# Cross-attention stack on one core: a new table of offsets for the hand-written order of all engines

## The reference, cut to what matters

```python
def _mha(x, kv, Wq, Wk, Wv, mask, causal):          # layer 0
    ...
    energy = jnp.einsum('bhsk,bhtk->bhst', Q, K)
    lengths = jnp.sum(energy[:, :, 0, :] != 0, axis=-1)
    energy = jnp.where(cols[None, None, None, :] >= lengths[:, :, None, None], -jnp.inf, energy)
    ...
    score = jax.nn.softmax(energy / jnp.sqrt(dk), axis=-1)
    out = jnp.einsum('bhst,bhtk->bhsk', score, V) * m
x = _L0_xattn_ref(x, ctx_1024, ...)   # attention 0, 1, feed-forward 256
x = _L1_xattn_ref(x, ctx_1024, ...)   # attention 2, 3, feed-forward 1024
x = _L2_xattn_ref(x, ctx_1024, ...)   # attention 4, heads of 64
x = _L3_xattn_ref(x, ctx_1024, ...)   # attention 5
```

## Time and profile before

| | us |
|---|---|
| median of 3 runs (2370.58 to 2371.80) | 2371.69 |
| the profiled execution | 2374.75 |
| its span, first to last instruction | 2373.0 |
| TensorE busy in it | 2331.2 |
| VectorE busy | 1498.0 |
| ScalarE busy | 1375.0 |
| GpSimd busy | 946.8 |

### The profile page before, as it was taken

The page is one execution under the profiler, slowest core; times in us unless marked ns, Lnnn a source line. Parts: engine busy times, 40 slices in busy tenths (PEclk is TensorE's granted clock), DMA queues, the critical chain, the costliest instruction groups (busy, mean ns, idle before and its releaser), DMA issues.

```text
span 2373.0 us, 74113 instructions
## 1 busy us (share of the span) xinstructions
PE 2331.2 (98%) x30353; PEld 1973.8 (83%) x30353; DVE 1498.0 (63%) x3091; ACT 1375.0 (58%) x3238; POOL 946.8 (40%) x1764
## 2 busy tenths in 40 slices
PE   8999999999999999999999999999999999999998
PEld 7788888888778888888877888888887788888887
DVE  6886654446888664444688766444478877544456
ACT  5566655545557665554655766554465675655545
POOL 3465422223457532223345743222334574322233
PEclk9999999999999999999999999999999999999999
DMA  5300000000100000000010000000001000000000
GB/s 184 111 2 3 2 2 1 1 1 16 40 5 2 3 2 2 1 1 1 18 40 3 2 3 3 1 1 1 1 24 34 2 2 3 2 1 2 1 1 20
DMA packets 23793, 32.51 MB, mean 14 GB/s; under 512 B 2304, under 2 KB 22176, under 8 KB 23328
## 3 DMA queue, kind: packets, MB, share of 16 engines
q1 hardware_dynamic: 23456, 27.78, 3.6%
HBM read 23.57 MB, written 4.19 MB: 12 GB/s over the span
## 4 chain that ended last, share of the span: by engine, by line
PE 90%; issue 4%; POOL 3%; DVE 2%; ACT 1%; DMA 0%; POOLq 0%; SPq 0%; DVEq 0%; ACTq 0%
PE M L582 52%; PE SC L778 14%; PE M L588 10%; PE M L812 6%; PE SC L794 3%; PE M L829 3%; PE SC L626 2%; POOL Kx L1339 1%; POOL Y L1375 1%; DVE nmax L1218 0%; ACT Pr L975 0%; POOL rstd L1390 0%; POOL q L1326 0%; POOL seen_diag L1366 0%; DVE Kx L1197 0%
## 5 line engine op out<-in xcount | busy, mean ns | idle before, releaser
L582 PE MATMUL M<-XT,W 128*128 128x128 f32 x4096 | 522.6, 277 | 1.0 <-DMA W<-w_k 0.9
L582 PEld LDWEIGHTS M<-XT,W 128*128 128x128 f32 x4096 | 491.5, 192 | 13.2 <-issue 2.0
L1218 DVE TENSOR_REDUCE nmax<-SC 128x8 f32<-128x1024 f32 x320 | 389.9, 1218 | 129.6 <-PE SC L778 129.3
L1339 POOL TENSOR_SCALAR Kx<-K,own,k_ones 128x128 f32<-128x128 f32 x640 | 294.4, 473 | 289.7 <-PE SC L778 214.0
L984 ACT ACTIVATE Pr<-SC 128x1024 f32<-128x1024 f32 x256 | 262.5, 1025 | 202.2 <-PE SC L778 201.3
L778 PE MATMUL SC<-Kx,Qx 32*128 32x128 f32 x5120 | 365.4, 280 | 13.7 <-issue 9.7
L778 PEld LDWEIGHTS SC<-Kx,Qx 32*128 32x128 f32 x5120 | 316.6, 186 | 68.1 <-issue 50.5
L778 PE MATMUL SC<-Qx,Kx 32*128 32x128 f32 x5120 | 372.2, 283 | 0.0
L954 ACT ACTIVATE Qx<-M,q_bias,q_scale 128x128 f32<-128x128 f32 x640 | 240.3, 457 | 148.1 <-PE M L582 148.1
L778 PEld LDWEIGHTS SC<-Qx,Kx 32*128 32x128 f32 x5120 | 310.9, 186 | 2.2 <-issue 0.7
L1414 POOL TENSOR_TENSOR Pr<-Pr,wrec 128x1024 f32<-128x1024 f32 x64 | 124.2, 1940 | 431.7 <-DVE wrec L1233 431.7
(11 more groups left out here) (145 smaller groups left out, 4074.2 us busy)
## 6 DMA issues: line engine op xcount, KB each, us to landing
X<-x SPq DMA_DIRECT2D x32, 128.0 KB, 2.1
c_in<-ctx_in SPq DMA_DIRECT2D x32, 128.0 KB, 2.3
out<-X SPq DMA_DIRECT2D x32, 128.0 KB, 1.7
RV<-row_vec SPq DMA_DIRECT2D x1, 2304.0 KB, 9.2
W<-w_k SPq DMA_DIRECT2D x5, 256.0 KB, 3.9
W<-w_q SPq DMA_DIRECT2D x5, 256.0 KB, 4.2
W<-w_v SPq DMA_DIRECT2D x5, 256.0 KB, 4.2
W<-w_f SPq DMA_DIRECT2D x1, 1024.0 KB, 6.2
```

The source lines that it names most:

```text
L582: last = pe.matmul(dst, a, b, start=(k == 0), stop=(k == len(lhsTs) - 1))
L1218: dve.tensor_reduce(nm, SC[h][:, :].rearrange("p (g c t) -> p g c t", c=KC, t=P), AX_X, ALU.max, negate=True).then_inc(maxima, 1)
L1339: last = pool.tensor_scalar(kx[:, half_of, c * P:(c + 1) * P], k[:, c * P:(c + 1) * P], own[:, half_of:half_of + 1], k_ones[:, half_of, c: ...
```

## The change

Only the numbers in `NARROW`, `OWN` and `BROAD` are new; the same instructions run, with the same waits, in other orders on TensorE, VectorE, ScalarE and GpSimd. On SyncE only the order in which DMAs stand can depend on slot times, and no offset of SyncE is changed. The diff, cut to two of the five narrow attentions:

```diff
-OWN = {0: dict(max=0.11, rXT=0.08, V=0.46, q0=-0.77, residual=2.68, exp=0.13, rE1=0.13, keys=-1.48, rPV=-0.16, K=-1.05,
-               rV=-0.08, MT=1.36, rK=0.06, rMT=-0.14, rQ=-0.03, XT=-1.497, L=-0.4, PV=2.951, seen0=-1.1, Q=-0.77,
-               CT=0.887, LN=3.34, LNe=0.34, rL=0.01, seen1=4, E1=3.08, rCT=0.02),
+OWN = {0: dict(XT=-1.456, rXT=-0.187, seen0=-1.418, CT=2.116, rCT=0.016, K=-1.012, rK=-0.393, keys=-0.654, Q=-0.714,
+               rQ=-0.106, V=-0.33, rV=0.231, q0=-0.946, L=-0.448, rL=0.15, max=0.108, exp=0.005, MT=1.188, rMT=-0.048,
+               PV=2.498, rPV=-0.2, E1=2.71, rE1=0.054, residual=2.874, LN=3.452, LNe=0.548, seen1=4.56),
...
-       2: dict(Q=-0.58, PV=2.56, rPV=0.34, rK=0.03, rV=0.14, V=0.163, keys=-0.92, rQ=0.05, LNe=0.38, max=0.08, K=-0.84,
-               rXT=0.03, MT=0.897, E3=3.68, E1=3.02, XT=-1.383, exp=0.06, rE2=0.07, E2=3.371, rMT=-0.07, LN3=0.14,
-               rCT=0.13),
+       2: dict(XT=-2.306, rXT=0.12, K=-1.158, rK=0.088, keys=-0.592, Q=-0.682, rQ=0.01, V=-0.288, rV=-0.152, max=-0.02,
+               exp=0.084, MT=1.006, rMT=0.026, PV=2.482, rPV=-0.032, E1=2.784, rE1=-0.04, E2=3.368, rE2=0.036, E3=4.26,
+               rE3=0.034, LN3=0.054, LNe=0.11),
...
```

More of the change, by code:

```diff
@@ L112, in wide @@
     return att(n) == WIDE
[L115 to L119, removed]
@@ L120 @@
-OWN = {0: dict(max=0.11, rXT=0.08, V=0.46, q0=-0.77, residual=2.68, exp=0.13, rE1=0.13, keys=-1.48, rPV=-0.16, K=-1.05,
-               rV=-0.08, MT=1.36, rK=0.06, rMT=-0.14, rQ=-0.03, XT=-1.497, L=-0.4, PV=2.951, seen0=-1.1, Q=-0.77,
-               CT=0.887, LN=3.34, LNe=0.34, rL=0.01, seen1=4, E1=3.08, rCT=0.02),
[L123 to L126, removed]
-       2: dict(Q=-0.58, PV=2.56, rPV=0.34, rK=0.03, rV=0.14, V=0.163, keys=-0.92, rQ=0.05, LNe=0.38, max=0.08, K=-0.84,
-               rXT=0.03, MT=0.897, E3=3.68, E1=3.02, XT=-1.383, exp=0.06, rE2=0.07, E2=3.371, rMT=-0.07, LN3=0.14,
-               rCT=0.13),
[L130 to L140, removed]
+NARROW = dict(XT=-1.2, TM=-1.5, SM=-1.25, K=-0.92, Q=-0.86, L=-0.42, V=0.3, CT=0.4, MT=0.86, PV=2.66, E1=3.2,
+              E2=3.54, E3=3.74, XF=4.4, F1=4.62, F2=4.9, seen0=-1.15, seen1=3.66, keys=-0.88, q0=-0.78,
+              mask_row=-0.3, residual=3.3, LN=3.4, T=1.5, H=0.5, rXT=0.03, rCT=0.03, rK=0.03, rQ=0.03, rL=0.03,
+              rV=0.03, rMT=0.03, rPV=0.03, rE1=0.03, rE2=0.03, rE3=0.03, rF1=0.03, rF2=0.03, max=0.12, exp=0.12,
+              LNe=0.25, LN3=0.06, LNf=0.05, rXF=0.03)
@@ new lines @@
+OWN = {0: dict(XT=-1.456, rXT=-0.187, seen0=-1.418, CT=2.116, rCT=0.016, K=-1.012, rK=-0.393, keys=-0.654, Q=-0.714,
+               rQ=-0.106, V=-0.33, rV=0.231, q0=-0.946, L=-0.448, rL=0.15, max=0.108, exp=0.005, MT=1.188, rMT=-0.048,
+               PV=2.498, rPV=-0.2, E1=2.71, rE1=0.054, residual=2.874, LN=3.452, LNe=0.548, seen1=4.56),
+       1: dict(XT=-1.496, rXT=0.293, TM=-2.964, SM=-2.156, K=-1.388, rK=0.258, keys=-1.056, Q=-0.622, rQ=-0.086,
+               V=-0.098, rV=0.06, q0=-0.946, L=-0.404, rL=0.064, max=0.068, exp=0.226, MT=1.15, rMT=0.134, PV=2.428,
+               rPV=-0.036, E1=2.926, rE1=-0.03, residual=2.9, LN=3.476, LNe=0.448, XF=3.948, rXF=0.12, F1=4.42,
+               rF1=-0.006, F2=4.798, rF2=-0.042, LNf=0.08),
+       2: dict(XT=-2.306, rXT=0.12, K=-1.158, rK=0.088, keys=-0.592, Q=-0.682, rQ=0.01, V=-0.288, rV=-0.152, max=-0.02,
+               exp=0.084, MT=1.006, rMT=0.026, PV=2.482, rPV=-0.032, E1=2.784, rE1=-0.04, E2=3.368, rE2=0.036, E3=4.26,
+               rE3=0.034, LN3=0.054, LNe=0.11),
+       3: dict(F2=5.282, XT=-2.294, rXT=0.009, mask_row=-1.232, K=-1.694, rK=0.074, keys=-0.238, Q=-0.936, rQ=0.046,
+               V=-0.098, rV=-0.33, max=-0.03, exp=0.086, MT=1.064, rMT=-0.186, PV=2.418, rPV=-0.036, E1=2.676, rE1=0.01,
+               E2=3.248, rE2=-0.02, E3=4.086, rE3=0.063, LN3=0.1, LNe=0.096, XF=4.61, rXF=-0.124, F1=4.958, rF1=0.003,
+               rF2=0.119, LNf=0.746),
+       5: dict(XT=-2.382, rXT=-0.084, K=-1.208, rK=0.156, keys=-0.784, Q=-0.834, rQ=-0.028, V=1.292, rV=0.06, max=0.144,
+               exp=-0.035, MT=1.076, rMT=0.01, PV=2.316, rPV=-0.134, E1=2.89, rE1=-0.006, E2=3.074, rE2=-0.022, E3=3.694,
+               rE3=0.021, LN3=0.242, LNe=0.528)}
@@ L143 @@
+BROAD = dict(XT=-1.398, Q=-0.354, Q1=0.142, K=-0.678, K1=0.284, S=0.028, S1=0.458, V=1.158, V1=0.912, TP=1.068,
+             TP1=1.23, PV=1.352, PV1=1.512, E3=2.14, sums=0.676, sums1=1.146, scale=0.57, scale1=1.186,
+             rXT=-0.138, rK=0.122, rQ=0.206, rV=0.074, rTP=-0.046, rPV=-0.025, max=0.12, exp=0.267, rE3=0.052,
+             LNe=0.618, LN3=0.122, rK1=0.136, rQ1=-0.034, rV1=0.108, rTP1=-0.008, rPV1=0.274, max1=0.24,
+             exp1=0.422)
 SETUP = {"ln1b": ("BT", "ln1b"), "f0": ("BC", "f0"), "lnfb": ("BT", "lnfb"), "q2": ("BC", "q2"), "k2": ("BC", "k2"),
```

## The result

| | before | after |
|---|---|---|
| median of 4 runs, us | 2371.23 | 2317.86 |
| lowest and highest | 2370.58, 2371.80 | 2317.53, 2318.61 |
| the profiled execution | 2374.75 | 2318.61 |
| its span | 2373.0 | 2316.8 |
| TensorE idle in the span | 41.8 | 18.2 |

The ratio is 0.9775, with a 95% interval of 0.9759 to 0.9792: 53.4 us faster by the medians, 56.1 by the two profiled executions. The prediction was 2329, with a range of 2307 to 2358.

What follows compares the result with a forecast made beforehand. The prediction took TensorE as the bound, VectorE next. From the profiled execution's 2374.75 it took 17.5 for fewer shape changes, 13.3 for L and 12 for other pauses, giving 2332.0; less 3.06, 2329 us, range 2307 to 2358.

Steps and rivals of the forecast that it cites:

- Part one: TensorE's queue: fewer returns from narrow pieces to whole-array work, 478 before and 389 after, saving 17.5 us.
- pieces next to pieces cost nothing: TensorE's queue: two kinds of narrow work in a row add no cost, read from PV taking 1.01 either way.
- Part two: L on TensorE waits for `q` from GpSimd, 15.3 us in all; about 2 stay, so 13.3 us go.
- Part three: TensorE's other pauses, 35.7 us, limited by VectorE: a third goes, -12 us, with bounds 0 and -35.7.
- the 92%: Attentions 0 and 1: TensorE assumed to wait once VectorE passes 92% busy, so 3.7 of 90 us can go.
- Moves with one answer: Side effects on PV, score steps, K copies, XT and SyncE loads, each checked against its cover and taken at zero.
- the 28 places with a cover of .07: Attention 0: 28 PVs stand 1.37 behind the step and need 1.3 for the exponentials; loss taken at zero.
- SyncE's late x loads: Attention 0: 12 x loads queue late behind CT, cover .7; taken at zero, 16 us at most.
- A: Rival: TensorE's pauses nearly all go, only 4 at the start and the tail's 2.8 stay; 2307 us, chance .15.
- B: Rival: pauses only change place, and the mode changes alone are left as gain; 2354 us, chance .15.
- C: Rival: slower than before, since PV waits for late exponentials on ScalarE, .53 at 58 PVs; 2385 us, chance .10.
- D: Rival: VectorE becomes slower with GpSimd working beside L1197, the length chain's end, costing 10 us; 2339 us, chance .10.

Runs made afterwards that it cites:

- x_l1: The new kernel with L of attention 1 alone moved up (offset -.56 for -.404): 2369.12 us, ratio 0.9988 to the kernel before.
- x_dve1: The new kernel with layer norm statistics done once more on VectorE in the 96 layer norms of attentions 0 and 1: 2321.60 us, ratio 0.9789.
- x_pvback: The new kernel with PV put back right behind the step at n + 2.5 in all narrow attentions: 2390.64 us, ratio 1.0079 to the kernel before.
- x_m5: The kernel before with the new offsets of attention 5 alone: 2421.09 us, ratio 1.0204.
- x_m0125: The kernel before with the new offsets of attentions 0, 1, 2 and 5, the old ones in attention 3 and the wide one: 2395.28 us, ratio 1.0106.

## Why the prediction was right, and where it wasn't

**The bound** held: TensorE before and after, and no engine took its place. That its clock was at the upper level throughout was true but for one stretch, 1.9 us.

**Part one, -17.5**: the prices give 2289.4 for the new list, and with the pauses of the trace all but 1.2 us of the span is accounted for (1.5 before). The reason given for one step was wrong (pieces next to pieces cost nothing: the change that was tested cost .107), and the sum didn't depend on it.

**Part two, -13.3**: L's pauses went from 15.3 to 1.7, -13.6. x_l1 shows the cause.

**Part three, -12** of 35.7: this is the term that was mis-sized. Those pauses fell by about 25, to some 11, with 2.8 of tail beside them; about 1.9 of the 25 is the stretch of lower clock, which the prediction did not see. The failed step is the 92%: "I take that TensorE begins to wait when VectorE passes 92%". VectorE is at 92.6% in the dense stretch, as the prediction's own sign for its forecast asked, and TensorE hardly waits; x_dve1 went to 95% for 3.7 us. The step before it failed too: with the pauses gone VectorE was to be busy 97%. It isn't, because the new order also spreads VectorE's work: no 85 us hold more than 79.0 of it, where the prediction put 79.4 into 81.9. Only 1.6 us of it left attentions 0 and 1 of the third round (126.2 us in 147.2 before, 124.6 in 140.6 after), so most of it moved within them. A share of a stretch says neither where the work may go nor which piece waits.

**Moves with one answer**: PV waits for exponentials 6 times, 1.6 us in all of which .8 at the tail, for 1 predicted, and never at the 28 places with a cover of .07. SyncE's late x loads cost .3 us on TensorE, once; the landing was 2.3 at the median and 4.8 at the longest. That PV in front of the step is cover for MT's way through VectorE was not seen: without it the score steps lose some 43 us in x_pvback, of which the trace gives 20.3 to Qx. That this did no harm to the sum is luck: it is an absence of waits in the new order, and the prediction had no term for it.

**The rivals**: the time lies halfway between the forecast (2329) and A (2307), and the range held it by A's side. A's condition, distances longer than what is needed at nearly every kind, was what held. B (waits change place) and C (late exponentials) didn't come. D (VectorE beside GpSimd) went the other way: L1198, the old L1197 of the earlier trace rows, takes 506 ns in the mean of 20 for 542:

```profile
L1198 DVE SCALAR_TENSOR_TENSOR Kx<-ne,spare_big,Kx 128x256 f32<-128x256 f32 x20 | 9.3, 506 | 0.4
```

Of the 53.4 us, then, the prices are 17.5, L 13.6, other waits about 25 (1.9 of it the lower clock), less 3 by which the profiled execution of before lay high.

## What to carry to other kernels

Where one engine is the bound and its queue is written by hand, count two things: changes between array shapes (here .1 each, and .1 more on going back to whole 32-bit work), and for each piece that waits the work between it and its producer against the time the producer's chain takes; the gain of a new order is the sum of both. A busy share of another engine, even 92%, is no ground to hold back a gain, as long as the distances are long enough. And an order of several in-order queues is one object: half of a better table can be slower than either whole, in good part by one copy that stands in front of an exponential in the queue of an engine that is busy 60%. Last, a long wait of the bound engine can cost more than itself: look at the granted clock behind it, in short stretches, since the slices of the page hide a fall of a few us.

## What the runs showed of the hardware

- A lone piece of 32 by 32 in the middle of whole 32-bit work costs .303 us, though it computes 32 columns; as the first of PV it costs .114, and a piece of PV's own shape there .007.
- A bf16 product of whole shape with 32 columns among 32-bit products costs .106, of which .08 lies on the products behind it. Why was not tested.
- TensorE's clock fell to the lower level in or soon behind waits of 2.1 us and more in x_l1, x_m5 and x_m0125, and once behind a wait of 1.4 in the kernel before. At that level a PVW took 1.90 us for 1.03 and a score step 2.01 for 1.10. Not every such wait had a fall behind it, and what decides was not tested; x_pvback, with 72.8 us more than the new kernel but no wait above 1.3 past the start, had none.
